# Output projections, norms and bf16 parts between the heads of a shared attention pass

## The reference, cut to what matters

```python
q = (x @ Wq + bq).reshape(1, B * N, H, hd)          # 16 heads of 16
kv = (cond @ Wkv + bkv)                             # all 8 tiles share one set of 1024 keys and values
...                                                 # q, k, v fake-quantised to 8 bits, softmax quantised to 0..255
x = layernorm(x + attn(q, k, v) @ Wp + bp)          # "out2", norm 5
...
g, u = x @ gate_w * gate_scale, x @ up_w * up_scale # fp8-rounded weights, 256 -> 768
x = layernorm(x + (silu(g) * u) @ down_w * down_scale)   # norm 6
```

## Time and profile before

| | us |
|---|---|
| median of 3 runs | 1478.36 |
| lowest, highest | 1475.77, 1478.98 |
| the profiled execution | 1475.77 |
| its span, first to last instruction | 1474.0 |

### The profile page before, as it was taken

The page is one execution under the profiler, slowest core; times in us unless marked ns, Lnnn a source line. Parts: engine busy times, 40 slices in busy tenths (PEclk is TensorE's granted clock), DMA queues, the critical chain, the costliest instruction groups (busy, mean ns, idle before and its releaser), DMA issues.

```text
span 1474.0 us, 24416 instructions
## 1 busy us (share of the span) xinstructions
PE 1293.9 (88%) x9109; PEld 854.9 (58%) x9114; DVE 1073.8 (73%) x2477; ACT 687.0 (47%) x1286; POOL 102.2 (7%) x95
## 2 busy tenths in 40 slices
PE   3777999999999999999999999988899598898576
PEld 1544766766766776676676676656777322222334
DVE  3647668857857857857867865744888899999477
ACT  1323633633643543553453463432444388888242
POOL 1111011001002002001001100000000000000001
PEclk9997999999999999999999999999999855555689
DMA  8300100100200200010010013002000099999100
GB/s 334 122 11 12 60 12 15 60 12 11 64 12 4 71 12 5 24 48 12 15 60 12 12 60 115 19 22 93 8 9 5 1 182 176 176 182 171 30 1 29
DMA packets 174517, 83.96 MB, mean 57 GB/s; under 512 B 137920, under 2 KB 170048, under 8 KB 173888
## 3 DMA queue, kind: packets, MB, share of 16 engines
q1 hardware_dynamic: 173248, 82.03, 23.0%
q10 hardware_dynamic: 1152, 0.36, 0.1%
HBM read 43.57 MB, written 5.24 MB: 33 GB/s over the span
## 4 chain that ended last, share of the span: by engine, by line
PE 57%; DVE 26%; issue 6%; ACT 4%; DMA 3%; POOL 2%; SPq 0%; DVEq 0%; POOLq 0%; ACTq 0%
PE ps_t L1657 11%; PE ps_p L1641 10%; PE ps_s L1877 7%; DVE w_moe L1530 7%; PE ps_o L1779 5%; PE ps_o L1771 4%; PE ps_o L1718 4%; PE ps_o L1877 3%; PE ps_p L1695 3%; DMA w_moe<-w_moe 3%; DVE probs L1116 3%; PE ps_s L1695 2%; PE ps_o L1722 2%; DVE row_max L1122 1%; DVE w_moe L1532 1%
## 5 line engine op out<-in xcount | busy, mean ns | idle before, releaser
L1657 PE MATMUL ps_t<-ident,probs 128*128 128x128 f32 x1072 | 169.1, 279 | 28.4 <-ACT probs L844 8.2
L844 ACT ACTIVATE probs<-probs 128x512 f32<-128x512 f32 x192 | 120.7, 628 | 147.0 <-DVE probs L1116 147.0
L1657 PEld LDWEIGHTS ps_t<-ident,probs 128*128 128x128 f32 x1072 | 122.3, 141 | 78.2 <-issue 38.0
L806 ACT ACTIVATE probsT<-ps_t 128x512 f32<-128x512 f32 x232 | 136.5, 589 | 55.2 <-PE ps_t L1657 55.1
L1877 PE MATMUL ps_s<-w_moe,xbT 128*128 128x352 f32 x352 | 123.5, 476 | 0.0
L1641 PE MATMUL ps_p<-w_qkv,xinT 128*128 128x512 f32 (+1 forms) x240 | 110.2, 586 | 8.1 <-DVE ropes L1145 6.5
L2050 PEld LDWEIGHTS ps_p<-vals,w_moe 128*128 128x128 f16 x1024 | 37.5, 106 | 121.8 <-DMA w_moe<-w_moe 103.6
L759 POOL TENSOR_TENSOR rms<-mean_sq,neg_half 128x8 f32<-128x8 f32 x40 | 67.1, 1678 | 268.6 <-DVE mean_sq L1149 268.6
L806 ACT ACTIVATE bigT<-ps_t 128x512 f32<-128x512 f32 (+1 forms) x128 | 68.7, 553 | 25.4 <-PE ps_t L1657 23.4
L1877 PEld LDWEIGHTS ps_s<-w_moe,xbT 128*128 128x128 f32 x352 | 64.8, 196 | 22.7 <-issue 2.5
L1718 PE MATMUL ps_o<-v_all,probsT 128*128 128x128 f32 x512 | 71.1, 282 | 7.6 <-DVE big L1179 7.6
(11 more groups left out here) (312 smaller groups left out, 2605.8 us busy)
## 6 DMA issues: line engine op xcount, KB each, us to landing
w_out<-in_wT_out SPq DMA_DIRECT2D x8, 2048.0 KB, 8.4
w_moe<-in_wT_gu SPq DMA_DIRECT2D x1, 5632.0 KB, 19.8
w_moe<-in_wT_down SPq DMA_DIRECT2D x1, 2816.0 KB, 26.2
w_qkv<-in_wT_qkv SPq DMA_DIRECT2D x1, 2048.0 KB, 9.7
keys<-keys2T SPq DMA_DIRECT2D x8, 256.0 KB, 2.0
keys2T<-keys SPq DMA_DIRECT2D x1, 2048.0 KB, 10.6
w_moe<-w_moe SPq DMA_TRANSPOSE x128, 3.3
w_qkv<-in_wT_qkv SPq DMA_DIRECT2D x2, 512.0 KB, 8.4
```

The lines of the kernel that those rows point to most:

```text
L806: nc.scalar.activation(dst, src.bitcast(BF16) if dst.dtype == BF16 else src, ACT.Copy)\
L844: nc.scalar.activation(probs[:, at % 4, :], probs[:, at % 4, :], ACT.Exp).then_inc(L0.exped, 1)
L1657: ins = nc.tensor.transpose(dst[:, i * P:(i + 1) * P], src(i), ident_b[:] if bf else ident[:])
```

## The change

The steps 1 to 5 of tiles 0 to 6 move into the shared pass, between the heads of the next tiles; tile 7 keeps them behind the pass, beside blocks 0 and 1. They no longer use ps_t: all of them work in the bank of ps_p that held the sums of their own tile (tile_bank(n)), and on semaphores of their own. With t the tile whose heads run:
- head 9: PE out_turn(t-1), ScalarE oq_take(t-1);
- head 12: PE out_project(t-1), behind the scores of that head and the sums of head 7;
- head 13: VectorE in5(t-1); head 14: out5(t-1);
- head 0: PE x5_turn(t-2), ScalarE x5_first(t-2); head 3: VectorE x5_rest(t-2); head 4: ScalarE x5_second(t-2); head 6: VectorE x5_last(t-2).

The sums of tile t wait for rest5 of tile t-2, which had the same bank. The two scalings of scales1 move ahead of the first head. The parts of tile 6 are finished right behind the last head, before take_shared(7). The number of matmuls, transposes, copies, VectorE and GpSimd instructions doesn't change.

```diff
+OQ_TURN, OQ_TAKE, OUT2, IN5, OUT5 = 9, 9, 12, 13, 14
+X5_TURN, X5_FIRST, X5_REST, X5_SECOND, X5_LAST = 0, 1, 3, 4, 6
-STARTED = [("oq", 0), ("oq", 1), ("oq", 2), ("x5", 0), ("oq", 3), ("x5", 1), ("x5", 2), ("x5", 3)]
-def beside(b):
-    return HT + b if b < HT else None, HT + b - 1 if 1 <= b <= HT else None
...
+        def tile_bank(n):
+            return ps_p[:, L1.p.at["av", n] % 2, 0:D]
...
+            def oq_take(n):
+                act.wait_ge(oq_turned, n + 1)
+                nc.scalar.activation(flat(lane_of(n).attT), tile_bank(n), ACT.Copy).then_inc(oq_taken, 1)
...
             for u in range(TILES * H1):
                 ...
+                if t >= 1 and h == OQ_TAKE:
+                    oq_take(t - 1)
+                if t >= 2 and h == X5_FIRST:
+                    x5_first(t - 2)
+                if t >= 2 and h == X5_SECOND:
+                    x5_second(t - 2)
...
             for b in range(2 * IB):
-                n, x = beside(b)
-                if n is not None:
-                    turned("oq", n, lane_of(n).attT, D)
                 gate(b)
+                if b == 0:
+                    oq_take(LAST)
                 fuse_parts(b)
-                if x is not None:
-                    x5_parts(x)
+                if b == 1:
+                    x5_first(LAST)
+                    x5_second(LAST)
...
+            for u in range(TILES * H1):
+                ...
+                if t >= 1 and h == TURN_LAG:
+                    take_shared(t - 1)
+                if t >= 1 and h == IN5:
+                    in5(t - 1)
+                if t >= 1 and h == OUT5:
+                    out5(t - 1)
+                if t >= 2 and h == X5_REST:
+                    x5_rest(t - 2)
+                if t >= 2 and h == X5_LAST:
+                    x5_last(t - 2)
+            x5_rest(LAST - 1)
+            x5_last(LAST - 1)
             take_shared(LAST)
...
+            def out_turn(n):
+                pe.wait_ge(heads_2, n + 1)
+                for k in range(KD):
+                    ins = nc.tensor.transpose(tile_bank(n)[:, k * P:(k + 1) * P], att2(n)[:, k * P:(k + 1) * P], ident[:])
+                ins.then_inc(oq_turned, 1)
+            def out_project(n):
+                pe.wait_ge(oq_taken, n + 1)
+                for k in range(KD):
+                    ins = nc.tensor.matmul(tile_bank(n), lane_of(n).attT[:, k, :], w_p2[:, k, :], start=(k == 0),
+                                           stop=(k == KD - 1))
+                ins.then_inc(out2_done, 1)
+            def x5_turn(n):
+                pe.wait_ge(N5.x_ready, n + 1)
...
                     if h == 0:
                         pe.wait_ge(L1.proj_taken, av - 1)
+                        if t >= 2:
+                            pe.wait_ge(rest5, t - 1)
...
+                t, h = u // H1, u % H1
+                if 1 <= t < TILES and h == OQ_TURN:
+                    out_turn(t - 1)
+                if 1 <= t < TILES and h == OUT2:
+                    out_project(t - 1)
+                if t >= 2 and h == X5_TURN:
+                    x5_turn(t - 2)
...
             for b in range(2 * IB):
-                n, x = beside(b)
-                if n is not None:
-                    out_turn(n)
                 gate_and_up(b)
-                if n is not None:
-                    out_project(n)
-                if x is not None:
-                    x5_turn(x)
+                if b == 0:
+                    out_turn(LAST)
+                    out_project(LAST)
+                if b == 1:
+                    x5_turn(LAST)
```

More of the change, by code:

```diff
@@ L210, in transposes1 @@
         keys += [("p", None if s is None else G1 * s + g) for g in (2, 3)] + [("qk1", p)]
[L211 to L214, removed]
     return [(key, n) for key, n in keys if n is not None]
@@ L223, in projections1 @@
     keys += [("av", t) for t in range(TILES)]
-    keys += [("out2", t) for t in range(TILES)] + [("down", t) for t in range(HT + 2)]
+    keys += [("down", t) for t in range(HT + 2)]
     return [(key, n) for key, n in keys if n is not None]
@@ L546, in decoder @@
         heads_2 = sem("heads_2")
+        oq_turned = sem("oq_turned")
+        oq_taken = sem("oq_taken")
+        out2_done = sem("out2_done")
+        x5_turned = sem("x5_turned")
+        second5 = sem("second5")
         parts5 = sem("parts5")
@@ L1414, in norm_in @@
                     link1(nc.vector.tensor_tensor(res, ps_t[:, t % 2, 0:D], scale, op))
+                elif key == "out2":
+                    dve.wait_ge(out2_done, t + 1)
+                    link1(nc.vector.tensor_tensor(res, tile_bank(t), add, op))
                 else:
@@ L1523, in take_shared, with x5_rest @@
                 nc.vector.tensor_tensor(att2(t), att2(t), v_scale[:], ALU.mult).then_inc(heads_2, 1)
[L1525 to L1535, removed]
+            def x5_rest(n):
+                dve.wait_ge(first5, n + 1)
+                nc.vector.tensor_tensor(tmp_tile(n), turned_tile(n), x5p[:, 0, :, n * P:(n + 1) * P], ALU.subtract)\
+                    .then_inc(rest5, 1)
@@ new lines, in x5_last, with in5, out5 @@
+            def x5_last(n):
+                cols = slice(n * P, (n + 1) * P)
+                dve.wait_ge(second5, n + 1)
+                nc.vector.tensor_tensor(x5p[:, 2, :, cols], tmp_tile(n), x5p[:, 1, :, cols], ALU.subtract)\
+                    .then_inc(parts5, 1)
+            def in5(n):
+                norm_in(N5, n, "out2", x4s[:, n], more=b_p2)
+            def out5(n):
+                norm_out(N5, n, x4s[:, n])
+            dve.wait_ge(ld_w["scales1"], 16)
+            link1(nc.vector.tensor_scalar(scales1[:, 2, :], scales1[:, 0, :], 0.5, None, ALU.mult))
@@ L1555, in fuse_last @@
                     .then_inc(fparts, 1)
[L1557 to L1572, removed]
             def in6(d):
@@ L1579, in out6 @@
                 norm_out(N6, d, lane_of(d).x6)
[L1581 to L1598, removed]
             for b in range(2 * IB):
-                n, x = beside(b)
                 d = b - IB - 2
                 gate_up_block(b)
-                if n is not None:
-                    in5(n)
+                if b == 0:
+                    in5(LAST)
                 if d >= 0:
@@ L1607, in _ @@
                 fuse_rest(b)
-                if n is not None:
-                    out5(n)
+                if b == 0:
+                    out5(LAST)
                 if d >= 0:
@@ L1612, in _ @@
                 fuse_last(b)
-                if x is not None:
-                    x5_rest(x)
-                    x5_last(x)
+                if b == 1:
+                    x5_rest(LAST)
+                    x5_last(LAST)
             in6(HT)
@@ L2024, in _ @@
             HEADS = TILES * H1
+            def out_turn(n):
[11 more added lines that the diff above has]
+                pe.wait_ge(N5.x_ready, n + 1)
+                for k in range(KD):
+                    ins = nc.tensor.transpose(tile_bank(n)[:, k * P:(k + 1) * P], x4s[:, n, k * P:(k + 1) * P], ident[:])
+                ins.then_inc(x5_turned, 1)
             for u in range(HEADS + SUM_LAG):
@@ L2055, in _ @@
                     ins.then_inc(out2 if h < H1 - 1 else L1.proj, 1)
-            pe.wait_ge(exp2, HEADS)
[L2059 to L2069, removed]
+                t, h = u // H1, u % H1
+                if 1 <= t < TILES and h == OQ_TURN:
[4 more added lines that the diff above has]
+                    x5_turn(t - 2)
+            pe.wait_ge(exp2, HEADS)
             def gate_and_up(b):
@@ L2097, in down @@
                 down_blocks(d, ps_p[:, at % 2, 0:D], range(IB)).then_inc(L1.proj, 1)
[L2099 to L2110, removed]
             for b in range(2 * IB):
-                n, x = beside(b)
-                if n is not None:
-                    out_turn(n)
                 gate_and_up(b)
-                if n is not None:
-                    out_project(n)
-                if x is not None:
-                    x5_turn(x)
+                if b == 0:
+                    out_turn(LAST)
+                    out_project(LAST)
+                if b == 1:
+                    x5_turn(LAST)
                 if IB < b <= IB + HT:
                     down(b - IB - 1)
-            pe.wait_ge(L1.trans_taken, L1.t.done(0, ("x5", LAST)))
             for d in (LAST - 1, LAST):
```

29 lines of the change are left out of this document (17 added, 12 removed).

## The result

| | before | after |
|---|---|---|
| median, us (16 runs each) | 1477.45 | 1473.53 |
| lowest, highest | 1474.12, 1479.48 | 1469.21, 1475.23 |
| the profiled execution | 1475.77 | 1475.11 |
| its span | 1474.0 | 1473.3 |
| mean granted PE clock | 0.903 | 0.899 |

The account below looks back on a forecast made before the run. VectorE, leading three near-full engines, was taken to bound the pass. Pass +27.3 us and stage behind -29.5 gave -2.2: 1473.6 from the profiled 1475.77, or 1476 against the median 1478.36; range 1465 to 1484.

Parts of the forecast that it names:

- VectorE leads, 1.38 us a head: In the shared pass: VectorE sets the pace of three near-full engines, 1.38 us from reduce to reduce.
- The inserted VectorE steps, 17.9 us: In the pass: in5, out5, x5_rest and x5_last are all on the path, 17.9 us more.
- The scalings, 0.4 us: Ahead of the first head: the two operations on scales1 cost at most 0.33 us each, 0.4 together.
- ScalarE's copies at nothing: In the pass: three 256-column copies per tile cost nothing; without cover, up to 0.46 us each.
- out_project stalls reduce 13 by 1.48 us: In the pass, head 12: the projection delays head 13's scores, VectorE stalls 1.48 us in seven tiles, 10.5 us more.
- Late transposes absorbed, -1.5 us: In the pass: VectorE waits from late DMA transposes shrink by 1.5 us, with ends 0 and -4.3.
- The turns wait without cost: In the pass, heads 9 and 0: out_turn and x5_turn wait on VectorE at no cost, x5_turn with 0.4 us to spare.
- gate_and_up(0) 20.0 us earlier: Behind the pass: gate_and_up(0) follows the last sums, at 1370.1 instead of 1390.14, 20.0 us less.
- Gate 0 to gate 6, 9.5 us less: Behind the pass: the stretch from block 0's gate to block 6's falls from 37.1 to 27.6 us.
- A: Rival, in the pass: the PE clock rises, the stall at reduce 13 vanishes, 10.5 us more gained, 1465; chance 0.15.
- B: Rival, in the pass: held turns out_turn and x5_turn land on VectorE, 7.7 us more, 1484; chance 0.14.
- C: Rival, behind the pass: the blocks run at 1.2 GHz, 3.3 us more, 1479; chance 0.06.

Follow-up runs that it names:

- e5: The kernel before with the sums six heads behind the scores instead of five (SUM_LAG = 6): 1467.66 us, ratio 0.9956 to before.
- e6: The changed kernel with the sums six heads behind the scores instead of five (SUM_LAG = 6): 1467.81 us, ratio 0.9970 to before.
- e4b: The changed kernel with the transposes of out_turn and x5_turn issued twice for tiles 0 to 6, run again for a trace: 1468.97 us, ratio 0.9979 to before.
- e1: The changed kernel with in5 moved from head 13 to head 12, ahead of reduce 13: 1467.15 us, ratio 0.9934 to before.
- e2: The changed kernel with in5 moved from head 13 to 12 and x5_last from head 6 to 12, ahead of in5: 1467.73 us, ratio 0.9929 to before.
- e3: The changed kernel with the matmuls of out_project issued twice for tiles 0 to 6: 1483.22 us, ratio 1.0033 to before.
- e9: The changed kernel with idle bf16 matmuls on the PE, three per head and longer bursts, to keep its clock up: 1511.97 us, ratio 1.0258 to before.

## Why the prediction was right, point by point

The forecast of a small gain was right: 2.2 us forecast, 3.9 measured. Step by step:

- **VectorE leads, 1.38 us a head**: right. Between insertions after keeps 1.38 us.
- **The inserted VectorE steps, 17.9 us**: right. The undisturbed tile shows 3.05 - 1.38 = 1.67 for in5 and 0.33 (1.71 or 1.70) for each of the others.
- **The scalings, 0.4 us**: right, 0.41 from the start of the first (1178.45) to the reduce.
- **ScalarE's copies at nothing**: right. In an undisturbed tile no head after a copy is longer than 1.38 us but for VectorE's own step.
- **out_project stalls reduce 13 by 1.48 us**: the mechanism and the place were right, the size was 1.58. I took 1.8 us for the projection, less than its row of 1.92 and without a reason; the scores behind it started 3.19 us after their predecessors instead of 3.08, and with the 1.92 of the row the sum would have given 1.60. 7 x 0.1 = 0.6 us more.
- **Late transposes absorbed, -1.5 us**: the term that was mis-sized. The loss by the distances fell from 5.4 to 1.3 us, so the change absorbed 4.1. By the profile's own waits, in which my term and its end of 4.3 were counted, it fell from 4.3 to 0.9 (11.4 less the seven waits of 1.5), which is 3.4. By either count it was more than twice my 1.5. I counted the heads with an insertion, five in sixteen. But the pauses act on all heads behind them: SyncE goes on issuing transposes at its own pace while VectorE makes no new exp possible for 1 to 1.6 us, and what was late is made up there. One such pause, from a moment of lateness:

```profile
1271.69 0.39 PE L2080 MATMUL ps_p<-vals,w_moe 128*128 128x16 f16 x8 [0.84 <-DMA w_moe<-w_moe]
```

  The PE waits 0.84 us for a transpose, as in the earlier trace rows, and here no reduce behind it waits at all. e5 and e6 show the size (5.1 us to be had in before, 1.3 in after); that it is SyncE's pace which catches up is argued, not shown.
- **The turns wait without cost**: right but for one tile. Where the PE was late already, in tile 1, reduce 10 waited 0.23 us behind out_turn, against my "no wait ahead of reduces 10 and 17" (e4b).
- **gate_and_up(0) 20.0 us earlier**: 31.65 less 11.97 is 19.7. Here luck helped: the same stretch took 10.4 to 13.0 us in the traces of e1, e2, e3 and e4b, whose code is the same there. It still waits for the last sums, which end 4.9 us ahead of gate 0, as forecast:

```profile
1398.60 0.38 PE L2080 MATMUL ps_p<-vals,w_moe 128*128 128x16 f16 x8 [0.68 <-DMA w_moe<-w_moe]
...
1399.21 4.64 PE L2105 MATMUL ps_s<-w_out,w_x 128*128 128x512 bf16 x11 [0.23 <-issue]
...
1403.89 0.69 ACT L1000 ACTIVATE squares<-ps_s,w_moe 128x512 f32<-128x512 f32 x1 [7.99 <-PE ps_s L2105]
...
1409.06 0.67 ACT L1000 ACTIVATE squares<-ps_o,w_moe 128x512 f32<-128x512 f32 x1
...
1414.80 0.67 ACT L1000 ACTIVATE squares<-ps_s,w_moe 128x512 f32<-128x512 f32 x1
...
1418.93 0.67 ACT L1000 ACTIVATE squares<-ps_o,w_moe 128x512 f32<-128x512 f32 x1
```

- **Gate 0 to gate 6, 9.5 us less**: 9.6. Blocks 0 and 1 take 5.17 and 5.74 us, the bare ones 4.13 to 4.16.

Sum: pass +24.9, scales +0.4, behind it -19.7 - 9.6: -4.0 us, and the medians say -3.9. That the two agree to 0.1 us is luck, since one trace gives the late transposes and gate 0 to about 1 us each. Of the 1.8 us by which the forecast was short, +0.6 is the stall, -2.6 the absorbed transposes, and the rest the last digits of the two terms behind the pass.

The forecast was right in its mechanism; its total is off mostly by one term, the late transposes.

Of the rivals, A didn't come: the clock stood at 0.50 from the first to the last head. B fell with e4b, but for 0.3 us. C fell too: the blocks ran at 0.94 on average and 4.15 us each. What the prediction said of in5 was true, "so it hides none of this", but I took the order as given and left unasked what the reverse would be worth. It is worth more than the change.

## What to carry to other kernels

Work that is moved under a full leading engine is paid there in full, as all 17.9 us were here, and the gain is then decided by the order inside the steps: put what the leading engine must do anyway (in5) in front of the operation that will wait, not behind it. Before crediting a change with a gain, look whether its pauses only hide a lateness that a longer lag would remove for nothing; try that digit in the kernel before as well. And price a step at both places: a tile cost 3.0 us beside the blocks and 3.6 in the pass as the change has it (4.2 where no late transpose hides under it).

## What the hardware showed that I had not expected

A PE busy all the time need not get its clock. In e9 it was busy 119.00 of 119 us and was granted 0.50, the 1.2 GHz level, with matmuls of 48 rows, of 16 and of 256 columns in turn; in after it had 0.50 for the 213 us of the pass at 88% busy. In e3, at the end of four of the seven doubled projections, it rose for a moment and fell again; the first time:

```profile
1221.20:1224.60 3.40, 2.35 (x31) 1.09 (x30) 3.16 (x9) 1.30 (x2) 0.13 (x1) 0.98 0.25 49
```

Ahead of these rises, and of the three of e9, the PE had run a projection, fp32 matmuls of 256 columns; but the other projections of e3 and e9, and all of after's, brought none. The Trainium skill ("TensorE: Matmul & The Clock Gate", Part 1) says that the array is throttled by default and that sustained matmul activity releases it. The rows of e9 don't agree: the profile has the PE busy for all of 119 us, and the granted clock stayed at 0.50. Why, no run here shows.

Most of the DMA transposes are on time, and some are late: the waits of the pass of before have

```profile
PE ps_p L2050 <- DMA w_moe<-w_moe: 11.8, 16, 1.6
```

The PE stood at 16 of the 128 sums, up to 1.6 us, of which VectorE feels 4.3 us in all; with one more head of lag the pass loses 0.3 us.
